# A perceiver kernel on one core: the state-space inputs reordered against GpSimd, GpSimd's products in quarters, one softmax in halves, idle products on TensorE

## The reference, cut to what matters

```python
x = x + mha16(ln(x), ctx, ctx)        # 16 heads of 16, causal against the last 128 of 2048 keys
x = x + selective_scan(ln(x))         # softplus step sizes, B and C rows, 16 states, y = sum(h*C) + D*x
x = x + lora_moe(ln(x))               # dense 256x256 and rank-16 experts, top 2 of 16
x = x + softmax(ln(x) @ ctx.T / 16 masked) @ ctx   # one head, key mask: "third attention" in the code
x = x + attention16(ln(x))            # projections, rope, local and compressed keys, sinks
x = x + expert_ffn(ln(x))             # 8 experts, three layers, top 2
```

## Time and profile before

| | |
|---|---|
| median of 3 runs | 515.98 us (515.32 to 516.42) |
| the profiled execution | 515.66 us, its span 513.7 us |
| TensorE matmuls, weight loads | 422.1 us busy (82%), 309.0 us (60%) |
| VectorE, ScalarE, GpSimd | 340.4 (66%), 275.5 (54%), 108.8 us (21%) |
| granted clock of TensorE, mean | 0.934 of full |
| slices (12.84 us each) in which it is 0.6 or lower | the 12th (from 141), the 17th (from 205) and the 19th (from 231) |
| GpSimd's two input products, L413 | 4.54 us each |

### The profile page before, as it was taken

How to read it: one execution, slowest core, us unless ns; L and a number is a source line. 1 busy time by engine, 2 the same in 40 slices (tenths; PEclk the granted TensorE clock), 3 DMA queues, 4 the chain that set the end, 5 groups by cost and what they waited for, 6 DMA issues and landing times.

```text
span 513.7 us, 9021 instructions
## 1 busy us (share of the span) xinstructions
PE 422.1 (82%) x3584; PEld 309.0 (60%) x3584; DVE 340.4 (66%) x544; ACT 275.5 (54%) x613; POOL 108.8 (21%) x76
## 2 busy tenths in 40 slices
PE   0269889978579888765999698998689789999997
PEld 0116556655346566325844373445579689999996
DVE  3698667775664977778236665684653599778772
ACT  4306797756438854553023242466784076777762
POOL 3010653010415100000001326250300113333300
PEclk9999999988858998586999999999799989999999
DMA  6598355661503037006230000005900197540000
GB/s 216 141 280 222 96 130 155 165 165 28 139 1 78 3 103 283 7 1 251 87 153 1 1 0 3 0 1 177 314 2 1 25 355 253 186 165 2 2 1 20
DMA packets 24329, 54.11 MB, mean 105 GB/s; under 512 B 5113, under 2 KB 13529, under 8 KB 20954
## 3 DMA queue, kind: packets, MB, share of 16 engines
q1 hardware_dynamic: 24288, 53.54, 33.6%
HBM read 40.65 MB, written 0.26 MB: 80 GB/s over the span
## 4 chain that ended last, share of the span: by engine, by line
PE 62%; DVE 19%; ACT 10%; issue 6%; DMA 1%; POOL 1%; SPq 0%; ACTq 0%; DVEq 0%; POOLq 0%
PE ps L1297 17%; PE ps L1105 8%; PE ps L918 6%; PE ps L905 5%; ACT reg_b L672 4%; PE ps L874 4%; DVE mx L1678 3%; PE ps L1262 2%; DVE reg_b L1467 2%; PE ps L1013 1%; PE ps L1251 1%; PE ps L1252 1%; PE ps L969 1%; PE ps L1032 1%; DVE bc_split L1451 1%
## 5 line engine op out<-in xcount | busy, mean ns | idle before, releaser
L1678 DVE TENSOR_REDUCE mx<-ps 128x1 f32<-128x1024 f32 x64 | 77.0, 1221 | 45.5 <-PE ps L874 28.9
L672 ACT ACTIVATE reg_b<-ps 128x512 f32<-128x512 f32 x128 | 75.4, 599 | 27.8 <-PE ps L905 16.8
L905 PE MATMUL ps<-qreg,reg_b 98*128 98x128 bf16 x512 | 50.9, 232 | 7.2 <-ACT reg_b L672 5.6
L905 PEld LDWEIGHTS ps<-qreg,reg_b 98*128 98x128 bf16 x512 | 37.6, 104 | 20.1 <-ACT reg_b L672 10.9
L1297 PE MATMUL ps<-part_a 128*128 128x256 f32 x384 | 48.2, 283 | 0.4 <-DVE part_a L1828 0.4
L1105 PE MATMUL ps<-reg_b,xT 128*128 128x512 f32 x96 | 47.6, 618 | 0.0
L1297 PEld LDWEIGHTS ps<-part_a 128*128 128x128 f32 x384 | 46.9, 192 | 0.6 <-DVE part_a L1828 0.6
L918 PE MATMUL ps<-reg_b 128*32 128x128 f32 x1024 | 45.6, 298 | 0.3 <-ACT reg_b L672 0.3
L385 POOL TENSOR_TENSOR rstd<-ve,cf 128x1 f32<-128x1 f32 x12 | 6.8, 565 | 183.6 <-DVE ve L1370 180.5
L874 PE MATMUL ps<-reg_b,qreg 96*128 96x512 bf16 x96 | 35.7, 442 | 11.2 <-DMA reg_b<-reg_b 7.6
L816 ACT ACTIVATE reg_a<-ps,b 128x256 f32<-128x256 f32 x64 | 30.2, 471 | 23.8 <-PE ps L1297 23.7
(11 more groups left out here) (280 smaller groups left out, 864.8 us busy)
## 6 DMA issues: line engine op xcount, KB each, us to landing
reg_b<-in_w SPq DMA_DIRECT2D x16, 512.0 KB, 7.6
reg_b<-in_w SPq DMA_DIRECT2D x8, 1024.0 KB, 7.0
reg_b<-reg_b SPq DMA_DIRECT2D x56, 128.0 KB, 3.3
reg_b<-in_w_qkv SPq DMA_DIRECT2D x3, 2048.0 KB, 7.5
reg_b<-reg_a SPq DMA_DIRECT2D x40, 128.0 KB, 3.2
reg_a<-in_ctxK SPq DMA_DIRECT2D x4, 1024.0 KB, 7.1
reg_a<-in_ctx SPq DMA_DIRECT2D x8, 512.0 KB, 4.8
reg_a<-in_ctxT SPq DMA_DIRECT2D x2, 2048.0 KB, 8.6
```

The source lines that it names most:

```text
L672: sc.activation(pT[n % 3], score_b[n % 2], ACT.Exp).then_inc(S("exp_done"), 1)
L905: mm = pe.matmul(cols, kS[g % 3][0:SROWS, c // 8, j, P * (c % 8):P * (c % 8 + 1)], qT[b][0:SROWS, HPG * hg + j, :], start=not last, stop=True)
L1678: ve.reduce_max(mx[:, piece // 2, piece % 2:piece % 2 + 1], score_a[m % 2].rearrange("p i k -> p (i k)"), X_AXIS).then_inc(S("max_done"), 1)
```

## The change

- VectorE: `split_maps(0)` changes places with `step_and_input(0)`; `normalise` is cut into `weigh_outputs` and `normalise`, and they and row 0's layer norm go to four successive pieces; in row 1's chain `lora_top(0)` comes before `step_and_input(1)`.
- GpSimd: `state_input` and `decay_exponent` each issue four products of four states instead of one of 16.
- ScalarE: the four `decay_exp` all lie in group 6; bc_copy 4 and 5 of row 1 come after all decay exponentials; row 0's `x` columns and `z` are copied two chunks later, as TensorE makes them.
- Third attention: the maximum and the exponential are taken in halves of 1024 keys, the two sums are added, the transposes wait for the half that they need; `compressed(0)` comes before row 1's maximum, and row 0's first half maximum before `scan(1, 1)`.
- TensorE: `keep_busy(i, count)` multiplies constants into the unused half of a bank, at ten places, 96 products of 128x256 bf16 together.

```diff
@@ -207 +207 @@
-        m3 = [sb(f"m3_{b}", [P, 4]) for b in range(NB)]
+        m3 = [sb(f"m3_{b}", [P, 7]) for b in range(NB)]
@@ -413,2 +413,4 @@
-                pool.tensor_tensor(state[0][:, h], tmp[0][:, h * P:(h + 1) * P].unsqueeze(1).to_broadcast([P, NS, P]),
-                                   bc_row[0][:, 0:NS, :], ALU.mult).then_inc(S("dbx_done"), 1)
+                for n in range(0, NS, 4):
+                    pool.tensor_tensor(state[0][:, h, n:n + 4],
+                                       tmp[0][:, h * P:(h + 1) * P].unsqueeze(1).to_broadcast([P, 4, P]),
+                                       bc_row[0][:, n:n + 4, :], ALU.mult).then_inc(S("dbx_done"), 1)
@@ -421,3 +423,5 @@
-                pool.tensor_tensor(decay[0][:, h], dt[0][:, P * h:P * (h + 1)].unsqueeze(1).to_broadcast([P, NS, P]),
-                                   ea[:, h, :].unsqueeze(2).to_broadcast([P, NS, P]), ALU.mult)\
-                    .then_inc(S("dta_done"), 1)
+                for n in range(0, NS, 4):
+                    pool.tensor_tensor(decay[0][:, h, n:n + 4],
+                                       dt[0][:, P * h:P * (h + 1)].unsqueeze(1).to_broadcast([P, 4, P]),
+                                       ea[:, h, n:n + 4].unsqueeze(2).to_broadcast([P, 4, P]), ALU.mult)\
+                        .then_inc(S("dta_done"), 1)
@@ -596 +600 @@
-                sc.wait_ge(S("dta_done"), h + 1)
+                sc.wait_ge(S("dta_done"), 4 * h + 2 * (half + 1))
@@ -625,3 +629,5 @@
-                sc.activation(p3[b].rearrange("p (i k) -> p i k", i=4), ps[:, 4 * b:4 * b + 4, :], ACT.Exp,
-                              bias=m3[b][:, 1:2], scale=1.0 / 16.0, accum_out=m3[b][:, 2:3])\
-                    .then_inc(S("p3_done"), 1)
+                for i in range(2):
+                    sc.activation(p3[b][:, 1024 * i:1024 * (i + 1)].rearrange("p (i k) -> p i k", i=2),
+                                  ps[:, 4 * b + 2 * i:4 * b + 2 * i + 2, :], ACT.Exp,
+                                  bias=m3[b][:, 1:2], scale=1.0 / 16.0, accum_out=m3[b][:, 2 + i:3 + i])\
+                        .then_inc(S("p3_done"), 1)
@@ -643,3 +649,3 @@
-                      (2, 13): [(late_query_rows, 3)], (3, 9): [(state_rates,)], (4, 1): [(weigh_masked, 0)], (4, 10): [(transposed_x, 1, 0)],
-                      (4, 12): [(copy_z, 0)], (5, 0): [(softplus_exp, 0)], (5, 1): [(softplus_log, 0)], (6, 4): [(decay_exp, 0, 0)],
-                      (6, 7): [(decay_exp, 0, 1)], (7, 1): [(decay_exp, 1, 0)], (7, 3): [(decay_exp, 1, 1)],
+                      (2, 13): [(late_query_rows, 3)], (3, 9): [(state_rates,)], (4, 1): [(weigh_masked, 0)], (4, 12): [(transposed_x, 1, 0)],
+                      (4, 14): [(copy_z, 0)], (5, 0): [(softplus_exp, 0)], (5, 1): [(softplus_log, 0)], (6, 3): [(decay_exp, 0, 0)],
+                      (6, 7): [(decay_exp, 0, 1)], (6, 10): [(decay_exp, 1, 0)], (6, 13): [(decay_exp, 1, 1)],
@@ -743,2 +748,0 @@
-            for i in range(4, 6):
-                bc_copy(1, i)
@@ -746 +750 @@
-            for i in range(6, 8):
+            for i in range(4, 8):
@@ -1017,2 +1021 @@
-                if part == 1:
-                    mm.then_inc(S("s3_ps"), 1)
+                mm.then_inc(S("s3_ps"), 1)
@@ -1021 +1023,0 @@
-                pe.wait_ge(S("p3_done"), b + 1)
@@ -1022,0 +1025 @@
+                    pe.wait_ge(S("p3_done"), 2 * b + i // 2 + 1)
@@ -1036,0 +1040,5 @@
+            def keep_busy(i, count):
+
+                for _ in range(count):
+                    pe.matmul(ps[:, i, 256:512], identb, cb[:, P:3 * P], start=True, stop=True)
+
@@ -1042 +1050,2 @@
-                      (2, 11): [(late_query_columns, 3)], (4, 9): [(misc_read, "o_all", 4), (x_to_columns, 1, 0)], (4, 11): [(step_sizes, 0)],
+                      (2, 11): [(late_query_columns, 3)], (4, 11): [(misc_read, "o_all", 4), (x_to_columns, 1, 0)], (4, 13): [(step_sizes, 0)],
+                      (5, 2): [(keep_busy, 6, 18)],
@@ -1164,0 +1174 @@
+            keep_busy(7, 4)
@@ -1165,0 +1176 @@
+            keep_busy(7, 5)
@@ -1166,0 +1178 @@
+            keep_busy(7, 6)
@@ -1168,0 +1181 @@
+            keep_busy(7, 2)
@@ -1169,0 +1183 @@
+            keep_busy(7, 14)
@@ -1170,0 +1185 @@
+            keep_busy(7, 3)
@@ -1173,0 +1189 @@
+            keep_busy(3, 8)
@@ -1174,0 +1191 @@
+            keep_busy(3, 4)
@@ -1180,0 +1198 @@
+            keep_busy(4, 32)
@@ -1413 +1431 @@
-            def normalise(b):
+            def weigh_outputs(b):
@@ -1420,0 +1439,3 @@
+
+            def normalise(b):
+                o = o_all[b][:, :, 0]
@@ -1466 +1487 @@
-                ve.wait_ge(S("dbx_done"), KD * b + h + 1)
+                ve.wait_ge(S("dbx_done"), 4 * (h + 1) if b == 0 else 4 * KD + h + 1)
@@ -1479 +1500 @@
-                ve.wait_ge(S("dta_done"), KD)
+                ve.wait_ge(S("dta_done"), 4 * KD)
@@ -1540,4 +1561,7 @@
-            def max3(b):
-                ve.wait_ge(S("s3_ps"), b + 1)
-                link(ve.reduce_max(m3[b][:, 0:1], ps[:, 4 * b:4 * b + 4, :].rearrange("p i k -> p (i k)"), X_AXIS))
-                ve.tensor_scalar(m3[b][:, 1:2], m3[b][:, 0:1], -1.0 / 16.0, None, ALU.mult).then_inc(S("m3_done"), 1)
+            def max3(b, half):
+                ve.wait_ge(S("s3_ps"), 2 * b + half + 1)
+                scores = ps[:, 4 * b + 2 * half:4 * b + 2 * half + 2, :]
+                link(ve.reduce_max(m3[b][:, 4 + half:5 + half], scores.rearrange("p i k -> p (i k)"), X_AXIS))
+                if half == 1:
+                    link(ve.tensor_tensor(m3[b][:, 0:1], m3[b][:, 4:5], m3[b][:, 5:6], ALU.max))
+                    ve.tensor_scalar(m3[b][:, 1:2], m3[b][:, 0:1], -1.0 / 16.0, None, ALU.mult).then_inc(S("m3_done"), 1)
@@ -1547,3 +1571,4 @@
-                ve.wait_ge(S("p3_done"), b + 1)
-                link(ve.reciprocal(m3[b][:, 3:4], m3[b][:, 2:3]))
-                link(ve.tensor_scalar(m3[b][:, 3:4], m3[b][:, 0:1], -8.0e30, m3[b][:, 3:4], ALU.is_gt, ALU.mult))
+                ve.wait_ge(S("p3_done"), 2 * (b + 1))
+                link(ve.tensor_tensor(m3[b][:, 6:7], m3[b][:, 2:3], m3[b][:, 3:4], ALU.add))
+                link(ve.reciprocal(m3[b][:, 6:7], m3[b][:, 6:7]))
+                link(ve.tensor_scalar(m3[b][:, 6:7], m3[b][:, 0:1], -8.0e30, m3[b][:, 6:7], ALU.is_gt, ALU.mult))
@@ -1551 +1576 @@
-                ve.scalar_tensor_tensor(x[b][:, :], bank(b, 0, D), m3[b][:, 3:4], x[b][:, :], ALU.mult, ALU.add)\
+                ve.scalar_tensor_tensor(x[b][:, :], bank(b, 0, D), m3[b][:, 6:7], x[b][:, :], ALU.mult, ALU.add)\
@@ -1665,3 +1690,3 @@
-            beside = {(0, 7): [(ln_stats, 0, 1)], (0, 8): [(ln_apply, 0, 1), (split_queries, 1)], (3, 8): [(masked_weight, 0)], (5, 2): [(normalise, 0)], (5, 3): [(ln_stats, 1, 0)],
-                      (5, 4): [(ln_apply, 1, 0)], (5, 8): [(step_magnitude, 0)], (6, 2): [(step_and_input, 0)],
-                      (6, 3): [(split_maps, 0)]}
+            beside = {(0, 7): [(ln_stats, 0, 1)], (0, 8): [(ln_apply, 0, 1), (split_queries, 1)], (3, 8): [(masked_weight, 0)], (5, 2): [(weigh_outputs, 0)], (5, 3): [(normalise, 0)],
+                      (5, 4): [(ln_stats, 1, 0)], (5, 5): [(ln_apply, 1, 0)], (5, 8): [(step_magnitude, 0)],
+                      (6, 2): [(split_maps, 0)], (6, 3): [(step_and_input, 0)]}
@@ -1700,0 +1726 @@
+            weigh_outputs(1)
@@ -1711 +1736,0 @@
-            step_and_input(1)
@@ -1712,0 +1738 @@
+            step_and_input(1)
@@ -1721,0 +1748 @@
+            max3(0, 0)
@@ -1723 +1750 @@
-            max3(0)
+            max3(0, 1)
@@ -1744 +1770,0 @@
-            max3(1)
@@ -1745,0 +1772,2 @@
+            max3(1, 0)
+            max3(1, 1)
```

More of the change, by code:

```diff
@@ L1710, in _ @@
             lora_hidden(0)
+            lora_top(0)
             step_and_input(1)
-            lora_top(0)
             lora_weighted(0)
```

## The result

The changed kernel takes 499.07 us, the median of four runs (496.72 to 502.26), against 516.2 us for the kernel before on the same chip. The ratio is 0.971 with a 95% interval of 0.966 to 0.977. The prediction was 497.2 (492.5 to 503.0).

What follows compares the result with a forecast made beforehand. TensorE, the busiest engine, was held by waits and its falling clock, over 20 us of it in groups 4 and 5. Terms -3.5 - 11.0 - 0.9 - 4.6 + 1.4 = -18.6 from 515.66 gave 497.1, with run offset 497.2 us (492.5 to 503).

Steps and rivals of the forecast that it cites:

- Group 5: First attention, group 5: split_maps(0) before step_and_input(0) removes the 7.27 us stall; small instructions stretch +2.3; -11.0 us, group 21.9.
- Group 4: First attention, group 4: normalise(0) cut and spread over successive maxima takes the group from 21.12 to 17.6 us, -3.5.
- the stall is spread: Group 4: TensorE's 2.57 us wait during normalise(0) becomes waits of 0.3 to 0.9 us.
- Groups 6 and 7: First attention: two ScalarE decay exponentials move from group 7 to 6; 0.7 each gained, 0.25 each lost; -0.9 us.
- Attention's end to outputs: First attention's end to third attention's outputs: scan 0.8 earlier, maximum 4.0 earlier, halved exponential 0.6; -4.6 us.
- Second row: Third attention, second batch row: compressed(0) ahead makes the maximum 1.1 later, halved exponential adds 0.3; +1.4 us.
- rival T: Third attention: transposes don't count as busy, so outputs begin at half clock, +1.2: 498.4 us; chance 0.05.
- Rival D: At the idle products' places on TensorE: they don't hold the clock, 501.5 us; chance 0.12.
- Rival C: End of group 5: wait for maximum rows grows to 3 us, clock falls, 0.9 + 4 more: 502 us; chance 0.15.
- B: Group 5's small instructions not held up (2.3), full clock for third attention's transposes (1.1): 493.8 us; chance 0.20.
- likeliest case: Whole kernel: the sum of the terms holds, 497.2 us within 494 to 500.5; chance 0.45.
- sign: Whole kernel: faster by over 0.2%, chance 0.96; slower 0.03; within 0.2% 0.01.

Runs made afterwards that it cites:

- e4: The kernel before with one edit, split_maps(0) ahead of step_and_input(0) on VectorE: 506.0 us, ratio 0.982.
- e5: e2 with GpSimd's four input and exponent products whole instead of in quarters: 498.83 us, ratio 0.966.
- e9: e2 with the maximum and the exponential of the third attention whole instead of in halves: 495.81 us, ratio 0.963.
- e7: e2 with 68 idle products in place of 32, and 44 more between row 1's two eights of transposes: 493.37 us, ratio 0.956.
- e6: e2 with compressed(0) back behind row 1's maxima of the third attention: 495.62 us, ratio 0.960.
- e3: The changed kernel without all 96 idle products: 502.82 us, ratio 0.975.
- e1: The changed kernel run once more, unchanged: 499.39 us, ratio 0.970.
- e2: The changed kernel with GpSimd's first expert casts also waiting for the second pair of normalised weights: 497.17 us, ratio 0.965.

## Why the prediction was right

*Group 5.* Right in its mechanism: e4 gives the larger part of it with one exchange. The stretch of the small instructions was 3.36 - 0.85 = 2.5 us for a predicted 2.3, a quarter cost 1.00 as taken, and the group 22.39 for 21.9. The rule of the Trainium skill ("SBUF — State Buffer", Who interferes with whom) puts the sum 0.5 higher, at +2.8; the trace lies between the two, and agrees in that all four were held, three at 0.95 to 0.97 and the first at 0.37 instead of 0.16. What the prediction's words left open was what quarters bring over whole products; e5 shows nothing.

*Group 4.* Right in size against the profiled execution (17.51 for 17.6). The credit is doubtful: e4 has 17.57 without the split. The step "the stall is spread" took the 2.57 us wait for a fixed property of `normalise(0)`, and part of it, 0.78 us, was one meeting with a GpSimd copy. How far the clock's fall behind it was chance stays open.

*Groups 6 and 7.* Wrong: 0 for -0.9. Group 7 gave back 0.78 as its two exponentials left, for a forecast of 1.4, and group 6 lost 0.76 for a forecast of 0.5: ScalarE went there from 13.19 of 15.72 to 14.79 of 16.48 us busy. It is the move of the exponentials: e4, which leaves them in their places, takes 15.45 and 16.98, and e5, with GpSimd's products whole, 16.48 and 16.19. The term that was mis-sized is the loss in group 6, 0.25 a piece, which measured 0.38, and the gain in group 7, 0.7 a piece, which measured 0.39.

*Attention's end to outputs.* -4.6 as predicted. The scan starts 0.96 sooner (0.8 predicted) and the maximum is ready 4.11 sooner (4.0). The step that placed the cause was only half right: the prediction has the 3.50 us wait go by the order of `bc_copy` on ScalarE, and e9 shows that this needs no split maximum. That it was this order, and not another edit of the chain, no run tests alone. Of the halves only 0.5 us is from the exponential. That the 32 idle products end too soon was right, and their place was worth 1.45 us at row 0's first output product and 2.5 us at its last, as e7 shows.

*Second row.* +2.05 for +1.4. From the end of row 0's outputs to the square-sums of the key rows it is +1.2, about what was laid out for VectorE's order, though e6 shows that taking the order back gains 2.6. The rest is that the outputs of row 0 took 7.92 instead of 7.07 us because they now began at the lower clock (7.31 in e3, 8.10 in e1; 7.07 at the full clock in e7). That part stood in no term. The clock's return behind idling differs: at 239.2 in the kernel before, 2.7 us after its transposes began, at 222.6 here, 5.1 us after. In both kernels' traces it can return while only fp32 transposes run. Here at row 1 these have run from 277.51 and the output products begin at 281.72 (windows of 0.5 us):

```profile
280.00:280.50 0.50, 0.50 (x4) 0.50 (x3) 0.00 (x0) 0.23 (x2) 0.00 (x0) 0.50 0.00 0
280.50:281.00 0.50, 0.50 (x6) 0.50 (x5) 0.00 (x0) 0.45 (x1) 0.00 (x0) 0.80 0.00 0
281.00:281.50 0.50, 0.50 (x7) 0.50 (x5) 0.00 (x0) 0.45 (x1) 0.00 (x0) 1.00 0.00 0
```

In e6 it returns at 278.6, with transposes alone since 275.15 and until 280.41:

```profile
278.50:279.00 0.50, 0.50 (x6) 0.50 (x5) 0.00 (x0) 0.30 (x2) 0.00 (x0) 0.88 0.00 0
```

So the rule of the Trainium skill that was weighed there ("TensorE: Matmul & The Clock Gate", Part 4), that transposes don't count as busy, does not agree with the measurement here. Of rival T the effect came, at row 0: the outputs began at the lower clock, for 0.85 us where T had 1.2. Its reason does not hold.

*Idle products.* Rival D falls: clock 1.00 in groups 4 to 7, and e3 without them is 502.8, near D's 501.5. Rival C is real in some executions: 4 of the 12 profiles that have the change in them, at 1.3 to 1.4 us, less than the 4.9 that C gave it. B fails because both its conditions do.

*What no step foresaw* is the -2.8 at the first expert, which is the luck of the two profiled executions. It may be why the profiled execution lies 2.35 us below the median, but that isn't shown (see e2). Without it the sum of the stretches is -16.2, and the medians differ by 17.1. The five terms of the forecast together gave -16.7 for -18.6: groups 6 and 7 fell short by 0.9, the second row by 0.65 and group 5 by 0.5. The likeliest case and the sign held, and the point forecast erred by 1.9 us.

## What to carry to other kernels

Move a small VectorE step ahead of whatever starts a long GpSimd instruction; one exchange of two entries gave 10.5 of 17 us here, while cutting the GpSimd work in quarters gave nothing, since a chain of four small steps meets four ends instead of one. Before splitting a step in halves, look whether its own engine is busy right up to it: if it is, halves move work and save none. Let idle products reach up to the end of the wait, and place them only where the wait's length is sure: 36 more gave 2.5 us here, and 44 behind a wait that had moved cost 5. And before crediting an edit with a few microseconds of one profile, look at the stretches ahead of the edit: here the clock alone made them differ by up to 3.5 us between executions.
